# Each scatter of sorted tokens waits for the landing of the scatter before it

## The chip, the cores and the metric

The kernel runs on one core of a Trainium2 chip. It is one launch, and the time is the device time of that launch in microseconds (us). The engines of the core are TensorE (PE in the rows, PEld for its weight loads), VectorE (DVE), ScalarE (ACT), GpSimd (POOL) and SyncE (SP, which here only starts transfers). They run their own instruction streams in order and meet through semaphores.

## The reference: two mixtures of experts, one behind the other

The input x has 8 sequences of 256 tokens with 128 features, all in fp32. Two layers are applied and the result is added to x.

The first layer works by sequence. Each sequence has logits for 8 experts; its two best experts are mixed with softmax weights, and one shared expert is added: gelu(x G) * (x U) times D, with 512 inner features.

The second layer works by token. It is the part that the change touches:

```python
h = (x - mu) / jnp.sqrt(var + LN_EPS) * ln_gamma + ln_beta
sw1, sw2 = (_bit_quant(shared_w1), _bit_quant(shared_w2))      # rounded to -1, 0, 1 times a scale
shared_out = jax.nn.silu(jnp.einsum('btd,fd->btf', h, sw1)) @ sw2.T
probs = jax.nn.softmax(h @ router_w.T, axis=-1)
top_prob, top_idx = jnp.max(probs, axis=-1), jnp.argmax(probs, axis=-1)
h1 = jax.nn.silu(jnp.einsum('btd,efd->ebtf', h, ew1))
eo = jnp.einsum('ebtf,edf->ebtd', h1, ew2)                     # 8 experts, 256 inner features
gate = jax.nn.one_hot(top_idx, N_EXPERTS) * top_prob[..., None]
routed_out = jnp.einsum('ebtd,bte->btd', eo, gate)
```

So every token of the second layer needs one shared expert and the one expert that its router picks.

## The kernel before

**Tiles.** The 2048 tokens are 16 tiles of 128 tokens, one token per partition. The first layer is a row of steps Q (16 for the shared expert, then 4 for each sequence), in which TensorE computes gate and up products (lines 447 to 449), ScalarE the gelu (718), VectorE the product (896) and the split of its result into two fp16 parts (902), and TensorE the down product (477 to 479), three steps later. Work of the second layer is threaded between these steps as the sequences become ready: VectorE's statistics, GpSimd's `deviation` (1270, 1272), ScalarE's `normalise` (764), TensorE's transposes `to_features` (495), ScalarE's features (771), TensorE's logits (502), VectorE's choice of expert (983 to 992). This runs over five parts: three of four tiles, two of two tiles.

**Sorting by expert.** The first 14 tiles go through the routed experts sorted by expert, in two groups: group 0 has tiles 0 to 7, group 1 has tiles 8 to 13. The last two tiles are computed for all eight experts instead (the dense units). For a group, TensorE's `ranks` and VectorE's `sort` give each token a row in a buffer in HBM, `sorted_scratch`, where each expert's rows begin at a multiple of 128; the row numbers are `slot_u` (1022). That buffer has 15 tiles of rows for group 0 and 13 for group 1 and was cleared with zeros early on.

**Scatters.** GpSimd then writes the group's normalised tiles to these rows, one tile with one indirect DMA (`scatter`, line 1275): 8 for group 0, 6 for group 1, each of 128 rows of 512 bytes, 64 KB. All scatters of a group count up one semaphore, by 16 each, and GpSimd issues them one after the other. Between the third and the fourth scatter of group 0 stands `deviation(2)`, behind the last one `deviation(3)`, and behind the last scatter of group 1 `deviation(4)`. Each is in GpSimd's order, so it starts only when GpSimd has got past what is in front of it.

**Loads and units.** SyncE waits until all scatters of a group have landed and loads the sorted rows back in four loads per group (`load_sorted`, line 401), one for each tile unit of three or four sorted tiles. Units 0 to 3 are of group 0, units 4 to 7 of group 1; the buffers of the latter lie in memory that the first layer's weights held, so the rows name them w. TensorE transposes a unit's tiles (`sorted_T`, line 587), ScalarE applies gamma and beta, VectorE splits the result, and TensorE runs the first layer (632), ScalarE the silu (836) and TensorE the second layer (657) with the expert's weights chosen by a register. In TensorE's order the transposes of unit j + 2 stand between the first layer of unit j and the second layer of the unit before it, so those of unit 4 come behind the first layer of unit 2. The transposes of units 0 and 1 come ahead of `ranks(1)`, on which the group 1 row numbers depend.

**Way back.** VectorE copies a unit's result out (1073), SyncE stores it (`store_routed`, 407), behind all eight loads in its order, and GpSimd gathers each tile's rows back with indirect DMAs (1284) when all stores of the group have landed, 8 and then 6. VectorE multiplies them by the gate and adds them (1179) at the very end, after the shared expert's last unit (617) and the four dense units (623, 830, 1085).

```python
            for t in range(GN[0]):
                scatter(0, t)
                if t == 2:
                    deviation(2)
            deviation(3)
            pool.wait_ge(slots_ready, 2)
            pool.wait_ge(norm_done, GP[1])
            for t in range(GN[1]):
                scatter(1, t)
            deviation(4)
```

Of the kernel before, what the change touches and what calls it, by code (L numbers as in the profile page):

```python
# [23 lines left out]
def moe_adaln_ffn(nc, x, cond, g_w, u_w, d_w, sg_w, su_w, sd_w, fs1, fs2, fe1, fe2, router, gamma, beta, out):  # L24
    B, S, D = x.shape
    E, _, I = g_w.shape
    NE, F, _ = fe1.shape
# [29 lines left out]
    NG = 2  # L57
    G0 = [0, 2 * NT]
    GN = [2 * NT, NT + NJ]
# [19 lines left out]
    with ExitStack() as ctx:  # L79
        def sb(name, shape, dt=F32):  # L80
            return ctx.enter_context(nc.sbuf_tensor(name, shape, dt))

        def sem(name):
            return ctx.enter_context(nc.semaphore(name))
# [84 lines left out]
        norm = sb("norm", [P, TT, P])  # L169
# [94 lines left out]
        tiles_ready = sem("tiles_ready")  # L264
        tile_scales = sem("tile_scales")
        cleared = sem("cleared")
        scattered = [sem(f"scattered{g}") for g in range(NG)]
        gathered = [sem(f"gathered{k}") for k in range(len(PIECES))]

        abs_done = sem("abs_done")  # L270
# [59 lines left out]
        def unit_rows(j):  # L330
            _, first, tiles = TILE_UNITS[j]
            return slice(first * P, (first + tiles) * P)
# [10 lines left out]
        def _(sp):  # L343
# [53 lines left out]

            def load_sorted(j):
                g, _, n = TILE_UNITS[j]
                sp.wait_ge(scattered[g], 16 * GN[g])  # L400
                sp.dma_start(hs_sb[j][:, 0:n, :],
                             sorted_dram[g][unit_rows(j)].rearrange("(i p) d -> p i d", p=P)).then_inc(hs_in[j], 16)

# [6 lines left out]
            for j in group_units(0):  # L410
                load_sorted(j)
            sp.wait_ge(out_taken, 2 * B)
            for j in group_units(1):
                load_sorted(j)
# [788 lines left out]
        def _(pool):  # L1203
# [68 lines left out]
                pool.tensor_tensor(shift[:, cols], neg_mean[:, cols], rstd[:, cols], ALU.mult).then_inc(rstd_done, 1)  # L1272

            def scatter(g, t):
                pool.indirect_dma_start(out=sorted_dram[g],  # L1275
                                        out_offset=bass.IndirectOffsetOnAxis(ap=slot_u[g][:, t:t + 1], axis=0),
                                        in_=norm[:, G0[g] + t, :], in_offset=None).then_inc(scattered[g], 16)

            def gather(k):
                g, first, last_tile = PIECES[k]  # L1280
# [18 lines left out]
# [4 lines that stand above are left out]
# [3 lines left out]
            for t in range(GN[1]):  # L1306
                scatter(1, t)
# [25 lines left out]
```

## Time and profile before

| what | value |
|---|---|
| time, median of 2 runs | 195.07 us (193.74 to 196.4) |
| time of the profiled execution | 195.82 us |
| its span | 194.1 us |
| TensorE, matmuls busy | 165.2 us (85%), 1615 instructions |
| VectorE busy | 137.2 us (71%) |
| ScalarE busy | 115.0 us (59%) |
| GpSimd busy | 85.6 us (44%) |
| scatters, line 1275 | 14, 14.9 us busy on GpSimd |
| gathers, line 1284 | 14, 13.3 us busy on GpSimd |
| mean granted TensorE clock | 0.979 of full speed |

The busy share of an engine is an average over stages that differ; it does not say which wait ends last in a given stage. The time of an indirect DMA on GpSimd is that of issuing it. Its data land later, and the row of GpSimd doesn't show that; a transfer that waits for it does, and so does the chain of waits.

### The profile page before, as it was taken

How to read it: one execution, taken by the hardware profiler on the slowest of the kernel's cores; microseconds unless marked ns; L12 is line 12 of the kernel's file. 1: busy time of each engine (PE TensorE's matmuls, PEld its weight loads, DVE VectorE, ACT ScalarE, POOL GpSimd, SP SyncE). 2: the span in 40 equal slices, each digit the busy share in tenths (PEclk: the TensorE clock that was granted, in tenths of full speed). 3: DMA queues.
4: the chain of work that ended last, by engine and by line, in shares of the span. 5: the costliest groups of instructions: out<-in, count | busy, mean ns of one | idle time of the engine just before them, and what ended most of it. 6: DMA issues, size and time to landing. Idle time of an engine off the chain costs nothing.

```text
span 194.1 us, 4961 instructions
## 1 busy us (share of the span) xinstructions
PE 165.2 (85%) x1615; PEld 147.2 (76%) x1615; DVE 137.2 (71%) x350; ACT 115.0 (59%) x281; POOL 85.6 (44%) x139
## 2 busy tenths in 40 slices
PE   0599899999999999899989989879688997559680
PEld 0369799999999999589879977658586996349580
DVE  0328999984689999978999973986753656321474
ACT  4328765664667696787943593855349883353330
POOL 5080000000999867980999766100860007707300
PEclk9999999999999999999999999999969999979998
DMA  3899369998000000000000011700118235231133
GB/s 114 291 340 289 128 203 297 301 341 250 6 14 19 14 17 17 2 19 14 3 14 17 27 30 54 196 12 0 43 41 224 64 96 135 57 95 41 41 113 108
DMA packets 26824, 19.83 MB, mean 102 GB/s; under 512 B 4712, under 2 KB 23536, under 8 KB 26800
## 3 DMA queue, kind: packets, MB, share of 16 engines
q1 hardware_dynamic: 25616, 17.38, 29.8%
q0 software_dynamic: 896, 1.84, 3.4%
q8 instruction: 15, 0.25, 0.5%
q10 hardware_dynamic: 288, 0.30, 0.5%
q14 instruction: 9, 0.07, 0.1%
HBM read 13.28 MB, written 5.64 MB: 97 GB/s over the span
## 4 chain that ended last, share of the span: by engine, by line
PE 37%; DVE 21%; issue 12%; another core or an unknown queue 7%; ACT 7%; DMA 6%; SPq 4%; POOL 3%; DVEq 0%; ACTq 0%; POOLq 0%
DVE a L902 6%; PE ps_out L461 6%; PE ps_up L657 4%; DMA region<-in_L_cond_skill_down 3%; DVE a_sb L896 3%; PE ps_up L447 3%; POOL sorted_scratch L1275 3%; PE ps_up L449 3%; PE ps_up L448 3%; PE ps_gate L447 3%; PE ps_gate L657 3%; PE ps_gate L449 2%; PE ps_gate L448 2%; ACT norm L764 2%
## 5 line engine op out<-in xcount | busy, mean ns | idle before, releaser
L718 ACT ACTIVATE g_sb<-ps_gate 128x512 f32<-128x512 f32 x48 | 28.4, 593 | 26.8 <-PE ps_gate L449 22.5
L896 DVE SCALAR_TENSOR_TENSOR a_sb<-g_sb,mix_w,ps_up 128x512 f32<-128x512 f32 x32 | 23.9, 746 | 10.7 <-PE ps_up L449 3.6
L447 PE MATMUL ps_gate<-x,w 128*128 128x256 f16 x96 | 26.8, 279 | 1.4 <-DVE x L872 1.4
L447 PE MATMUL ps_up<-x,w 128*128 128x256 f16 x96 | 26.8, 279 | 1.4 <-DVE a L896 0.7
L448 PE MATMUL ps_up<-x,w 128*128 128x256 f16 x96 | 26.8, 279 | 0.4 <-issue 0.3
L449 PE MATMUL ps_up<-x,w 128*128 128x256 f16 x96 | 26.8, 279 | 0.0
L448 PE MATMUL ps_gate<-x,w 128*128 128x256 f16 x96 | 26.8, 279 | 0.0
L449 PE MATMUL ps_gate<-x,w 128*128 128x256 f16 x96 | 26.8, 279 | 0.0
L477 PE MATMUL ps_out<-w,a 128*128 x128 | 23.6, 219 | 1.0 <-DVE a L902 0.6
L1284 POOL DMA_INDIRECT routed<-routed_scratch,slot_u x14 | 13.3, 953 | 24.3 <-DMA routed_scratch<-w 20.6
L478 PE MATMUL ps_out<-w,a 128*128 x128 | 23.3, 219 | 0.0
L479 PE MATMUL ps_out<-w,a 128*128 x128 | 23.3, 219 | 0.0
L724 ACT ACTIVATE a<-a_sb 128x512 f16<-128x512 f32 x32 | 20.0, 624 | 5.2 <-DVE a_sb L896 5.2
L866 DVE SCALAR_TENSOR_TENSOR w<-region,w 128x512 f16<-128x512 f32 x26 | 17.4, 682 | 7.6 <-ACT w L702 6.0
L902 DVE TENSOR_TENSOR a<-a_sb,a 128x512 f16<-128x512 f32 x32 | 22.7, 709 | 0.0
L1275 POOL DMA_INDIRECT sorted_scratch<-norm,slot_u x14 | 14.9, 1065 | 13.0 <-DVE slot_u L1022 9.2
L1237 POOL TENSOR_SCALAR scales<-sums 128x3 f32<-128x3 f32 x9 | 2.7, 297 | 36.5 <-ACT abs_junk L753 35.8
L657 PE MATMUL ps_up<-region 128*128 128x128 f32 (+1 forms) x124 | 17.3, 298 | 0.0
L461 PE MATMUL ps_out<-w,a 128*128 128x128 f32 x128 | 16.9, 275 | 0.0
L657 PEld LDWEIGHTS ps_up<-region 128*128 128x128 f32 x124 | 16.6, 215 | 0.2
L836 ACT ACTIVATE region<-ps_gate,tile_scale 128x128 f32<-128x128 f32 x32 | 9.3, 377 | 11.6 <-remote 6.6
L461 PEld LDWEIGHTS ps_out<-w,a 128*128 128x128 f32 x128 | 15.6, 192 | 0.2
(148 smaller groups left out, 403.1 us busy)
## 6 DMA issues: line engine op xcount, KB each, us to landing
region<-in_L_cond_skill_gate SPq DMA_DIRECT2D x8, 256.0 KB, 4.0
region<-in_L_cond_skill_up SPq DMA_DIRECT2D x8, 256.0 KB, 4.4
region<-in_L_cond_skill_down SPq DMA_DIRECT2D x8, 256.0 KB, 5.0
x_tok<-in_x SPq DMA_DIRECT2D x4, 256.0 KB, 6.6
f_raw<-in_L_ffn_expert_w SPq DMA_DIRECT2D x1, 1024.0 KB, 11.2
routed_scratch<-w SPq DMA_DIRECT2D x4, 256.0 KB, 2.6
sorted_scratch<-zeros SPq DMA_DIRECT2D x1, 960.0 KB, 10.5
sorted_scratch<-zeros SPq DMA_DIRECT2D x1, 832.0 KB, 10.3
```

Of the source, the lines that this page charges most:

```text
L447: pe.matmul(dst, w16[:, w_cols(e, 0, col)], x16[:, 0, xs], start=True, stop=False)
L448: pe.matmul(dst, w16[:, w_cols(e, 0, col)], x16[:, 1, xs], start=False, stop=False)
L449: last = pe.matmul(dst, w16[:, w_cols(e, 1, col)], x16[:, 0, xs], start=False, stop=True)
L461: last = pe.matmul(ps_out[batch % 2][:, t * P:(t + 1) * P], a32[:, Q % 4, m * S + t * P:m * S + (t + 1) * P], sd_32[Q % 2][:, m * P:(m + 1 ...
L477: pe.matmul(dst, hi, w16[:, w_cols(e, 0, col)], start=first and t == m == 0, stop=False)
L478: pe.matmul(dst, hi, w16[:, w_cols(e, 1, col)], start=False, stop=False)
L479: last = pe.matmul(dst, lo, w16[:, w_cols(e, 0, col)], start=False, stop=final and t == m == 1)
L657: last = pe.matmul(ps_y[u % 2][:, t * P:(t + 1) * P], s, w, start=c == 0, stop=c == FC - 1)
L718: act.activation(g_sb[:, Q % 2, :], ps_gate[Q % 2][:, :], ACT.Gelu_apprx_tanh, scale=1.0 / WS).then_inc(gelu_done, 1)
L896: dve.scalar_tensor_tensor(out=dst, in0=g_sb[:, Q % 2, :], scalar=weight, in1=ps_up[Q % 2][:, :], op0=ALU.mult, op1=ALU.mult).then_inc(pro ...
L902: dve.tensor_tensor(a16[:, Q % 4, 1, :], a_sb[:, Q % 2, :], a16[:, Q % 4, 0, :], ALU.subtract).then_inc(alo_done, 1)
L1275: pool.indirect_dma_start(out=sorted_dram[g], out_offset=bass.IndirectOffsetOnAxis(ap=slot_u[g][:, t:t + 1], axis=0), in_=norm[:, G0[g] + ...
```

## The change

The one semaphore per group on which the scatters counted becomes two, used in turn: even scatters count on the first, odd ones on the second. Every scatter but the first of a group waits, on GpSimd, until the scatter in front of it has counted its 16, so until that one has landed. SyncE's loads wait for both semaphores of the group, for half of the scatters on each. Nothing else differs; the scatters, their order and their data are the same.

```diff
--- before.py
+++ after.py
@@ -264,7 +264,7 @@
         tiles_ready = sem("tiles_ready")
         tile_scales = sem("tile_scales")
         cleared = sem("cleared")
-        scattered = [sem(f"scattered{g}") for g in range(NG)]
+        scattered = [[sem(f"scattered{g}_{k}") for k in range(2)] for g in range(NG)]
         gathered = [sem(f"gathered{k}") for k in range(len(PIECES))]
 
         abs_done = sem("abs_done")
@@ -397,7 +397,8 @@
 
             def load_sorted(j):
                 g, _, n = TILE_UNITS[j]
-                sp.wait_ge(scattered[g], 16 * GN[g])
+                for k in range(2):
+                    sp.wait_ge(scattered[g][k], 16 * GN[g] // 2)
                 sp.dma_start(hs_sb[j][:, 0:n, :],
                              sorted_dram[g][unit_rows(j)].rearrange("(i p) d -> p i d", p=P)).then_inc(hs_in[j], 16)
 
@@ -1272,9 +1273,12 @@
                 pool.tensor_tensor(shift[:, cols], neg_mean[:, cols], rstd[:, cols], ALU.mult).then_inc(rstd_done, 1)
 
             def scatter(g, t):
+
+                if t >= 1:
+                    pool.wait_ge(scattered[g][(t - 1) % 2], 16 * ((t - 1) // 2 + 1))
                 pool.indirect_dma_start(out=sorted_dram[g],
                                         out_offset=bass.IndirectOffsetOnAxis(ap=slot_u[g][:, t:t + 1], axis=0),
-                                        in_=norm[:, G0[g] + t, :], in_offset=None).then_inc(scattered[g], 16)
+                                        in_=norm[:, G0[g] + t, :], in_offset=None).then_inc(scattered[g][t % 2], 16)
 
             def gather(k):
                 g, first, last_tile = PIECES[k]
```

## Rows read from the trace of the kernel before

**Rows 1.** The page, part 4: the ended-last chain by line, share of the span.

```profile
DVE a L902 6%; PE ps_out L461 6%; PE ps_up L657 4%; DMA region<-in_L_cond_skill_down 3%; DVE a_sb L896 3%; PE ps_up L447 3%; POOL sorted_scratch L1275 3%; PE ps_up L449 3%; PE ps_up L448 3%; PE ps_gate L447 3%; PE ps_gate L657 3%; PE ps_gate L449 2%; PE ps_gate L448 2%; ACT norm L764 2%
```

**Rows 2.** Chain of waits, 142 to 148 us: start us, us, what.

```profile
142.39 2.24 DMA sorted_scratch<-norm,slot_u
...
144.69 3.00 DMA w<-sorted_scratch
...
147.74 0.33 PE ps_out L587
```

**Rows 3.** TensorE's time line: start, us, engine, line, instruction, count [idle before <-releaser].

```profile
115.43 0.44 PE L495 MATMUL ps_b<-ident,norm 128*128 128x128 f32 x2 [0.52 <-ACT norm L764]
...
131.82 1.07 PE L587 MATMUL ps_out<-ident,hs_sb 128*128 128x128 f32 x8
...
141.36 0.94 PE L632 MATMUL ps_up<-region 128*128 128x128 f16 x8 [1.52 <-issue]
...
142.73 3.00 PE L657 MATMUL ps_up<-region 128*128 x16
...
146.96 0.67 PE L632 MATMUL ps_up<-region 128*128 128x128 f16 x8 [0.26 <-ACT region L836]
...
148.24 1.95 PE L657 MATMUL ps_gate<-region 128*128 x16
```

**Rows 4.** Busy us by stretch: PE, PEld, DVE, ACT, POOL, then granted clock, DMA.

```profile
141.00:147.00 6.00, 5.08 (x36) 4.67 (x37) 3.52 (x11) 3.25 (x11) 2.95 (x4) 0.72 0.28 86
147.00:153.00 6.00, 5.79 (x57) 5.28 (x58) 2.71 (x5) 5.79 (x19) 0.00 (x0) 1.00 0.66 181
```

**Rows 5.** GpSimd's time line, group 0 scatters.

```profile
107.12 1.38 POOL L1275 DMA_INDIRECT sorted_scratch<-norm,slot_u  x1 [0.31 <-POOL f_raw L1261]
...
112.35 1.05 POOL L1270 TENSOR_TENSOR rstd<-var_e,neg_half 128x4 f32<-128x4 f32 x1 [1.18 <-DVE neg_mean L970]
113.47 0.20 POOL L1272 TENSOR_TENSOR shift<-neg_mean,rstd 128x4 f32<-128x4 f32 x1
...
117.70 1.48 POOL L1275 DMA_INDIRECT sorted_scratch<-norm,slot_u  x1 [0.30 <-issue]
119.49 0.96 POOL L1275 DMA_INDIRECT sorted_scratch<-norm,slot_u  x1 [0.30 <-issue]
125.26 0.73 POOL L1270 TENSOR_TENSOR rstd<-var_e,neg_half 128x2 f32<-128x2 f32 x1 [4.82 <-DVE neg_mean L970]
```

**Rows 6.** GpSimd's time line, group 1 scatters, first and last of six.

```profile
135.75 1.03 POOL L1275 DMA_INDIRECT sorted_scratch<-norm,slot_u  x1 [9.20 <-DVE slot_u L1022]
...
142.39 0.96 POOL L1275 DMA_INDIRECT sorted_scratch<-norm,slot_u  x1 [0.30 <-issue]
```

**Rows 7.** SyncE's DMA queue, time line, the group 0 loads.

```profile
121.77 2.02 SPq L401 DMA_DIRECT2D hs_sb<-sorted_scratch  x4
```

**Rows 8.** VectorE's time line.

```profile
117.66 0.69 DVE L1061 TENSOR_TENSOR region<-h_all,region 128x512 f16<-128x512 f32 x1
...
135.29 0.17 DVE L1022 TENSOR_SCALAR slot_u<-slot_f 128x6 uint32<-128x6 f32 x1
...
189.98 1.66 DVE L1179 SCALAR_TENSOR_TENSOR x_tok<-routed,prob,x_tok 128x128 f32<-128x128 f32 x6
```

**Rows 9.** Chain of waits, pieces without a known releaser.

```profile
118.35 2.85 another core or an unknown queue
...
161.64 3.77 another core or an unknown queue
...
167.54 3.82 another core or an unknown queue x2
...
178.78 3.27 another core or an unknown queue
```

**Rows 10.** The loads of group 0's sorted tiles, issue to landing.

```profile
DMA to landing us min/median/max: 3.0/3.7/4.0
```

**Rows 11.** GpSimd's time line, the last gather.

```profile
181.12 0.95 POOL L1284 DMA_INDIRECT routed<-routed_scratch,slot_u  x1 [0.30 <-issue]
```

## The prediction

> **What bounds the kernel now.** I read the page first. Its chain by line is a list of many VectorE and TensorE lines, and one entry is the scatter itself, "POOL sorted_scratch L1275 3%" [rows 1]. So the line that the change touches is on the path that ends last; the next question is where. I then read the chain of waits in order of time around the group 1 scatters [rows 2]. It runs without a gap from the last scatter: issued at 142.39 us, landed 2.24 us later, SyncE starts the load of sorted tokens at 144.69, that load lands 3.00 us later, and TensorE's transposes of that unit start at 147.74. TensorE had finished the work in front of them a moment earlier (146.96 + 0.67 = 147.63 [rows 3]), and everything for the remaining units is queued behind them. So whatever makes the last scatter of group 1 land later comes out at TensorE one for one. After 147.74 TensorE has hardly any idle time (5.79 of 6 us busy [rows 4]), and from there the chain goes through the units one after the other to the end. Nothing in it waits for a clock time, so a delay at 147.74 is not given back by itself.
>
> The time lines of GpSimd give the scatters' beat [rows 5, 6]. An undisturbed scatter keeps GpSimd 0.96 us and the next starts 0.30 us after that, one every 1.27 us, while the last one needs 2.24 us from its start to its landing [rows 2]. Today the landing of one overlaps the issue of the next.
>
> **The price of one wait.** With the change, scatter t starts when scatter t-1 has landed, plus the time that GpSimd needs to wake and start. The landing: 2.24 us [rows 2]; group 0 confirms it, its last scatter starts at 119.49 and the load that waits for it at 121.77, 2.28 us later [rows 5, 7]. The start after a wait: slot_u ends at 135.29 + 0.17 = 135.46 and the scatter that waited for it starts at 135.75 [rows 8, 6], 0.29 us. So a beat is 2.24 + 0.29 = 2.53 us in place of 1.27, 1.26 us more. Bounds: 0.97 us if the start is already prepared when the landing comes (2.24 - 1.27), and 1.78 us if each scatter also takes 1.48 us instead of 0.96, as the slow one at 117.70 did [rows 5] (1.26 + 0.52). I take 1.26: 10 of the 14 scatters lie within 0.1 us of 0.96.
>
> **Group 1, on the path.** Six scatters, five waits. Today they start from 135.75 to 142.39, 6.64 us apart in all [rows 6]. Then 5 x 2.53 = 12.65 us, so the last starts and lands 6.0 us later, and load and transposes follow. No cover: TensorE waits for this load already [rows 2, 3]. With the two bounds: 5 x 2.24 - 6.64 = 4.6 us, and 5 x 3.05 - 6.64 = 8.6 us.
>
> **Group 0, beside the path except at one point.** Seven waits. The first scatter takes 1.38 us, 0.42 more than the others, so the third starts at 107.12 + 0.42 + 2 x 2.53 = 112.6 and leaves GpSimd at 113.56. In GpSimd's order the reciprocal deviation of part 2 (line 1270) is queued behind the third scatter. Today it waits for VectorE and starts at 112.35 [rows 5]; then it starts at 113.56, 1.2 us later. ScalarE's normalise needs its result, the shift that ends at 113.67 today, and TensorE's transposes of part 2 wait 0.52 us for that normalise at 115.43 [rows 5, 3]. Both are queued in front of the last expert work, so 1.2 us goes to TensorE here and on to the group 1 slots. Bounds: 0 (the slip vanishes in the 2.85 us that this chain later spends on "another core or an unknown queue" [rows 9]) and 1.7 (a third scatter of 1.48 us). I take 1.2.
>
> The rest of group 0 is hidden. Scatter 3 starts 0.29 us behind the shift, at 113.67 + 1.2 + 0.29 = 115.16, the last 4 x 2.53 later at 125.28, and lands at 127.5 against 121.7 today. The loads follow; landing takes 3.7 us in the median and 4.0 at most [rows 10], so unit 0's tokens are there at 131.3. What hides it is the last work of the expert layers: TensorE comes to these transposes at 131.82 [rows 3], then at 133.0 with the slip. If that cover were gone, up to 5.8 us would be on the path. The deviation of part 3, queued behind the last scatter, would find GpSimd free at 126.24; its input from VectorE comes at 125.26 today [rows 5] and 126.4 with the slip, so it adds nothing. The deviation of part 4, behind the last scatter of group 1, goes to the dense tiles, whose transposes stand behind the stalled unit on TensorE: nothing.
>
> **SyncE.** Each of the eight loads has one more wait, on a semaphore that is already full when the other one is; I cost it at nothing, between 0 and the 0.06 us that lie today between landing (142.39 + 2.24 = 144.63) and issue (144.69) [rows 2]. The routed stores stand behind the group 1 loads on SyncE and are late with them, but the gathers wait for the last store of a group, whose data come from the delayed TensorE anyway. The last gather leaves GpSimd at 182.07 [rows 11] and, with a scatter's 1.28 us from there to the landing, is in at 183.4; VectorE wants it at 189.98 [rows 8], and both sides move together: nothing.
>
> **TensorE's clock.** The stall at the group 1 transposes grows from 0.1 to about 6 us. What holes can do is in the trace: behind TensorE's idle 1.52 us before 141.36, the stretch 141 to 147 has a mean granted clock of 0.72, so part of it ran at 1.2 GHz instead of 2.4, and the same 16 matmuls took 3.00 us there and 1.95 us in the next unit [rows 3, 4]. I expect one further slow stretch behind the new stall. Price: 3.00 - 1.95 = 1.05 us for the second-layer matmuls of a unit, and up to 0.3 for a half of the first layer (0.94 against 0.67). Part of the slow time may fall into the stall, so I take 1.0; bounds 0 and 1.9.
>
> **The sum.** 6.0 + 1.2 + 1.0 = 8.2 us. The profiled execution took 195.82 us (its span 194.1) and would take 204.0; the median of the two runs is 195.07, 0.75 us lower, so the forecast is 203.3 us.
>
> A rule of the Trainium skill speaks against the change: "DMA: Bandwidth & Descriptors", section "Rules for kernel authors", advises to issue a transfer early, compute, and wait late, since the fixed cost then overlaps. The trace agrees, with 1.27 us a scatter against 2.24 for a landing. The same page, section "Anatomy of one DMA — SWDGE (gpsimd) path", fits 2.0 us plus bytes over 436e3; for 64 KB that gives 2.15 us, an estimate by which group 1 would cost 5.5 us and the forecast be 202.8.
>
> **Rivals.**
>
> *A, the forecast* (203.3 us).
>
> *B, the slip of group 0 is swallowed.* Before 121.2 the chain holds 2.85 us of unexplained waiting while scatters are being issued [rows 9, 5]. If scatters one at a time disturb the other engines less, this shrinks, and then the group 1 slots are bound by unit 1's tokens: 127.6 + 0.5 + 4.0 = 132.1, its transposes end at 132.6, against 131.82 + 1.07 = 132.9 today. So 6.0 - 0.3 + 1.0 = 6.7 and 201.8 us. For it: the wait has no releaser in the trace. Against: no such wait is seen at the first five scatters either.
>
> *C, slow scatters.* The scatter at 117.70 took 1.48 us while VectorE subtracted two SBUF tiles from 117.66 on [rows 5, 8]. Today this is half hidden; in a serial row every such delay is paid. At 0.52 us each, group 1 costs 2.6 us more (205.9); group 0's five scatters behind the deviation put its tokens at 133.9, 0.9 past their cover: 206.8 us. Against: most scatters ran undisturbed beside VectorE's work. The Trainium skill, "SBUF — State Buffer", section "Who interferes with whom", says that a VectorE instruction with two inputs in SBUF and a GpSimd instruction that reads SBUF lock each other out; by that rule this rival would be the usual case in group 0.
>
> *D, the other side: the units behind the stall lose their unexplained waits.* From 161 to 182 the chain has 3.77 + 3.82 + 3.27 = 10.9 us on "another core or an unknown queue", ScalarE waiting while GpSimd issues gathers [rows 9, 11]. They are larger than the whole cost, and I can't say what makes them. If the shifted meeting of stores, gathers and units removed them all, 203.3 - 10.9 = 192.4 us. It decides from 4.3 us removed (203.3 - 199.0); with the 2.85 us of group 0 gone too, 189.6, which would be faster. Against: gathers and units move by the same delay, so they meet as before.
>
> *E, the change does not do what it says*: each landing is over before the next scatter could start anyway, 195 us. The 2.24 us against the beat of 1.27 excludes it, unless that landing is the last one's alone.
>
> **How the numbers follow.** Chances: A 0.53, B 0.16, C 0.12, D 0.17, E 0.02. What a measurement of this kernel can tell from no change is about 2%, 191.2 to 199.0 us; the two runs shown differ by 1.4%. A with its own bounds (4.6 to 8.6, 0 to 1.7, 0 to 1.9) covers 199.7 to 207.3. The range goes from 199.0 to 207.5 and holds A, B and C, leaving out D and E, 0.19. Slower by over 2%: A, B, C, 0.81. Faster: the extreme of D, 0.04. Within 2%: the rest, 0.15.
>
> **What the profile after would show.** GpSimd's scatters 2.4 to 2.6 us apart in both groups, each ended by a DMA landing; line 1270 of part 2 at about 113.6; the first group 0 load at 127.5 with no TensorE wait at its transposes; the last group 1 scatter 12.6 us after the first; TensorE idle about 6 us in front of the transposes of unit 4, released by the load; a stretch at the lower clock right behind it; the units from there to the end as long as today. The prediction fails if the beat is below 2.2 us, if TensorE waits at unit 0 already, or if the stretch from unit 4 to the end changes by more than 3 us.

## The result: 209.25 us, slower, and above the range

The changed kernel took 209.25 us in the median of 2 runs (207.88 to 210.63) against 195.07 us: a ratio of 1.070, with a 95% interval of 1.063 to 1.076. The direction was right and the size was not; 203.3 us was forecast, 207.5 at most. Ratios and intervals, here and below, are worked out from the fast runs of both kernels and medians from all runs, so a ratio can differ a little from the quotient of two medians. The profiled execution took 210.63 us, with a span of 208.8, so 14.7 us more than the span of 194.1 before. The two runs are a thin base: in later sets of six runs the same kernel was 1.042 and 1.039 times as long as the one before.

**The scatters on GpSimd's time line**, columns as in [rows 5]; they answer to [rows 5, 6]:

```profile
106.98 1.38 POOL L1279 DMA_INDIRECT sorted_scratch<-norm,slot_u  x1 [0.31 <-POOL f_raw L1262]
...
112.58 0.96 POOL L1279 DMA_INDIRECT sorted_scratch<-norm,slot_u  x1 [1.54 <-DMA sorted_scratch<-norm,slot_u]
113.56 1.06 POOL L1271 TENSOR_TENSOR rstd<-var_e,neg_half 128x4 f32<-128x4 f32 x1
...
122.88 1.48 POOL L1279 DMA_INDIRECT sorted_scratch<-norm,slot_u  x1 [2.51 <-DMA sorted_scratch<-norm,slot_u]
127.63 0.96 POOL L1279 DMA_INDIRECT sorted_scratch<-norm,slot_u  x1 [3.27 <-DMA sorted_scratch<-norm,slot_u]
130.14 0.96 POOL L1279 DMA_INDIRECT sorted_scratch<-norm,slot_u  x1 [1.55 <-DMA sorted_scratch<-norm,slot_u]
131.13 0.73 POOL L1271 TENSOR_TENSOR rstd<-var_e,neg_half 128x2 f32<-128x2 f32 x1
...
141.74 1.03 POOL L1279 DMA_INDIRECT sorted_scratch<-norm,slot_u  x1 [9.61 <-DVE slot_u L1023]
...
154.39 0.96 POOL L1279 DMA_INDIRECT sorted_scratch<-norm,slot_u  x1 [1.53 <-DMA sorted_scratch<-norm,slot_u]
```

Each scatter now waits for a landing. In group 1 the first and the last are 12.65 us apart, to the hundredth what was forecast. In group 0 the last one starts at 130.14 us instead of the forecast 125.28, and the deviation of part 3 behind it at 131.13.

**The chain of waits** (start us, us, what), where it enters the scatters and where it leaves them; it answers to [rows 2]:

```profile
112.58 3.63 DMA sorted_scratch<-norm,slot_u
...
116.49 2.31 DMA sorted_scratch<-norm,slot_u
...
119.07 3.54 DMA sorted_scratch<-norm,slot_u
...
122.88 4.49 DMA sorted_scratch<-norm,slot_u
...
131.13 0.74 POOL rstd L1271
...
141.28 0.18 DVE slot_u L1023
...
154.39 2.23 DMA sorted_scratch<-norm,slot_u
...
156.71 2.75 DMA w<-sorted_scratch
```

What the reader is to see: the chain goes through group 0's scatters as well, which it didn't before, and three of their landings take 3.5 to 4.5 us instead of 2.3. From the last scatter it goes by the deviation, ScalarE's normalise, TensorE and VectorE to group 1's row numbers. The page's chain by line says the same in one entry, against 3% for the scatters in [rows 1]:

```profile
DMA sorted_scratch<-norm,slot_u 13%; PE ps_gate L658 7%; PE ps_out L462 6%; PE ps_up L658 5%; DVE a L903 4%; DMA region<-in_L_cond_skill_down 3%; PE ps_up L448 2%; PE ps_up L450 2%; PE ps_up L449 2%; PE ps_gate L448 2%; PE ps_gate L449 2%; PE ps_gate L450 2%; POOL sorted_scratch L1279 2%; PE ps_out L588 2%; DVE a_sb L897 2%
```

**TensorE's time line**, answering to [rows 3]; in brackets its idle time and what ended it:

```profile
133.10 0.44 PE L496 MATMUL ps_b<-ident,norm 128*128 128x128 f32 x2 [4.16 <-ACT norm L765]
134.86 1.01 PE L618 MATMUL ps_gate<-region 128*128 128x512 f16 x2 [1.32 <-ACT region L827]
...
137.23 1.95 PE L588 MATMUL ps_out<-ident,hs_sb 128*128 128x128 f32 x8
138.97 0.25 PE L525 MATMUL ps_b<-chosen_e,earlier 128*128 128x56 f16 x1
...
159.50 1.12 PE L588 MATMUL ps_out<-ident,w 128*128 128x128 f32 x4 [9.29 <-DMA w<-sorted_scratch]
160.41 3.62 PE L658 MATMUL ps_gate<-region 128*128 x16
...
165.27 1.95 PE L658 MATMUL ps_up<-region 128*128 x16
```

TensorE is idle for 4.16 us ahead of part 3's transposes, where no hole was forecast, and for 9.29 us ahead of unit 4's. Behind each hole the matmuls take nearly twice their time: the second layer of a unit 3.62 us and later 1.95, the eight transposes of sorted tokens 1.95 us against 1.07 in [rows 3]. In the kernel before, part 3's transposes and the start of `ranks(1)` (524 there, 525 here), on which group 1's row numbers depend, are these rows:

```profile
128.81 0.39 PE L495 MATMUL ps_b<-ident,norm 128*128 128x128 f32 x2
...
133.06 0.20 PE L524 MATMUL ps_b<-chosen_e,earlier 128*128 128x56 f16 x1 [0.18 <-DVE chosen_e L992]
```

From the one to the other it is 4.25 us before and 5.87 after (133.10 to 138.97), at a mean granted clock of 1.00 before and 0.54 after. The stretch around the second hole, columns as in [rows 4] (the granted clock stands ahead of the DMA share):

```profile
154.00:159.50 5.50, 0.00 (x1) 0.00 (x1) 0.00 (x0) 0.88 (x2) 1.89 (x3) 0.50 0.33 98
159.50:165.00 5.50, 5.50 (x35) 5.44 (x36) 0.94 (x2) 1.00 (x2) 0.00 (x0) 0.57 0.43 118
165.00:173.00 8.00, 8.00 (x89) 7.97 (x88) 4.46 (x13) 7.45 (x25) 0.00 (x0) 1.00 0.35 93
173.00:209.00 36.00, 24.13 (x177) 21.48 (x174) 15.54 (x45) 11.36 (x31) 13.42 (x14) 0.85 0.28 79
```

While TensorE has nothing to do the grant is 0.50, the 1.2 GHz level; in the 5.5 us after it the mean is 0.57, and only then full speed. In the last 36 us the mean is 0.85: there are slow stretches again.

**Where the 14.7 us are**, by the same four points in both spans:

| stretch | before | after | difference |
|---|---|---|---|
| to `slot_u` of group 1 | 135.29 | 141.28 | +6.0 |
| first to last scatter of group 1 | 6.64 | 12.65 | +6.0 |
| from the last scatter to unit 4's transposes | 5.35 | 5.11 | -0.2 |
| unit 4's transposes to the end of the span | 46.4 | 49.3 | +2.9 |

The sum of the rows, with 0.46 us between `slot_u` and the first scatter in both, is the difference of the spans. SyncE's queue shows the group 0 loads, which answer to [rows 7]:

```profile
132.44 2.02 SPq L402 DMA_DIRECT2D hs_sb<-sorted_scratch  x4
```

They start 10.7 us later than in [rows 7], and VectorE's row numbers, in the chain above at 141.28, 6.0 later than in [rows 8].

### The profile page after: what moved, and what is told of

The parts are those of the page before. It is cut to its first block, busy times and chain, and to the rows that moved or that the text cites. A ratio compares the mean times of both kernels' runs of the same rounds, so it can differ in the third digit from the quotient of the medians.

```text
span 208.8 us, 4968 instructions
## 1 busy us (share of the span) xinstructions
PE 168.8 (81%) x1615; PEld 151.7 (73%) x1615; DVE 136.9 (66%) x350; ACT 115.3 (55%) x281; POOL 85.5 (41%) x139
## 4 chain that ended last, share of the span: by engine, by line
PE 45%; DMA 18%; DVE 16%; issue 10%; SPq 4%; ACT 3%; POOL 3%; DVEq 0%; POOLq 0%
DMA sorted_scratch<-norm,slot_u 13%; PE ps_gate L658 7%; PE ps_out L462 6%; PE ps_up L658 5%; DVE a L903 4%; DMA region<-in_L_cond_skill_down 3%; PE ps_up L448 2%; PE ps_up L450 2%; PE ps_up L449 2%; PE ps_gate L448 2%; PE ps_gate L449 2%; PE ps_gate L450 2%; POOL sorted_scratch L1279 2%; PE ps_out L588 2%; DVE a_sb L897 2%
## 5 line engine op out<-in xcount | busy, mean ns | idle before, releaser
L658 PE MATMUL ps_gate<-region 128*128 128x128 f32 (+1 forms) x116 | 18.6, 327 | 0.0
L658 PEld LDWEIGHTS ps_gate<-region 128*128 128x128 f32 x116 | 18.0, 241 | 0.5 <-issue 0.3
L658 PE MATMUL ps_up<-region 128*128 128x128 f32 (+1 forms) x124 | 16.5, 289 | 0.0
```

The lines of the kernel that those rows point to most:

```text
L658: last = pe.matmul(ps_y[u % 2][:, t * P:(t + 1) * P], s, w, start=c == 0, stop=c == FC - 1)
```

## Why some landings are slow

In the trace a scatter is 32 packets, 16 of 4096 bytes and 16 of 4 bytes, and it has landed when the last of them has. The DMA queues of two short stretches of the changed kernel, each around a slow landing, against one around an ordinary landing (queue and kind: packets, MB, share of 16 engines). At 113.8 to 115.6 us, the third scatter (3.63 us):

```profile
q0 software_dynamic: 32, 0.07, 12.2%
q8 instruction: 1, 0.02, 4.3%
```

At 124.6 to 126.9 us, the sixth (4.49 us, of which 1.48 for issuing it):

```profile
q0 software_dynamic: 32, 0.07, 9.6%
q8 instruction: 1, 0.02, 4.4%
```

At 127.6 to 129.6 us, the seventh, landed in 2.2 us:

```profile
q0 software_dynamic: 32, 0.07, 10.2%
```

Beside each slow landing there is one packet of an engine's own instructions on the DMA engines (for the fifth scatter, 3.54 us, one of queue 14), and beside the ordinary one there is none. In each of the three slow scatters 30 of the 32 packets start within 0.34 us; the other two, one of 4096 and one of 4 bytes, come later, the last of them 1.4, 1.0 and 1.8 us after the first. Over all 14 scatters of the profiles of the changed kernel, the kernel before and the sixteen runs below, 252, it is the same: in 213 the last packet started 0.33 to 0.43 us after the first, and no instruction packet overlapped any of them; in 39 it started 0.49 us or more after, and an instruction packet overlapped every one. While the landings are hidden behind the next issue this costs nothing. One of the 39 is in the trace of the kernel before, the third scatter of group 1 (138.59 us), beside an instruction packet at 139.93, and no row of the prediction has it; in a serial row each one is paid in full. The Trainium skill, "Runtime: NRT & Kernel Launch", section "Instruction fetch mechanics", says that an engine's sequencer fetches 16 KiB blocks over a DMA queue of its own and that the cost of crossing into the next block is mostly hidden. The trace agrees on the block for queue 8 (15 packets carry 0.25 MB); what such a fetch costs another transfer that something waits for, the section doesn't say, and here it is 1.4 us for the third scatter (3.63 for 2.24).

## The experiments

One thing has to be known to read the times. The kernel before takes 186 us in three of the sets of runs and 195 to 197 in the other one and in the first comparison. Each of the four sets ran on a chip of its own, so these are called faster and slower chips below; whether it is the chip or the moment isn't shown. A profile of it from a slower chip has stretches of 2.6 to 3.9 us in the chain that end with no known releaser, 14.1 us together; the profiles of its nearest relatives from the faster chips (with `ranks(1)` moved, and with two scatters in flight) have none. So every kernel here is compared only with the kernel before on the same chip.

### Which group costs what

In `scatter`, the wait in one group only; the loads wait as in the changed kernel.

```diff
-                if t >= 1:
+                if g == 1 and t >= 1:
```

> Waits in group 1 only. Theory Q (the wait is dear in group 0 because GpSimd's deviation of part 3 is queued behind the last scatter, and group 0's landings are slower than 2.24 us): the last scatter of group 1 starts 12.65 us after the first instead of 6.64, and TensorE's hole in front of unit 4 grows from 0 to 6 us and is followed by a stretch at the lower clock. 6.0 + 1 to 1.9, so 202 to 203 us. Theory H (the prediction: group 0 is hidden but for 1.2 us) expects the same here. Theory N (each wait costs the same, wherever it is): 5 of 12 waits, 14.2 x 5/12 = 5.9, so 201.0 us.

192.04 us against 186.41, ratio 1.036 (1.029 to 1.043). GpSimd's time line:

```profile
134.33 1.03 POOL L1279 DMA_INDIRECT sorted_scratch<-norm,slot_u  x1 [9.86 <-DVE slot_u L1023]
...
146.93 0.96 POOL L1279 DMA_INDIRECT sorted_scratch<-norm,slot_u  x1 [1.54 <-DMA sorted_scratch<-norm,slot_u]
```

12.60 us from the first to the last: the same row as in the changed kernel, and 5.6 us of cost by the medians, 5.3 to 7.9 by the interval. The term of 6.0 us for group 1 holds. Whether the clock adds 1 to 1.9 us the interval leaves open, and this run alone doesn't tell theory N (5.9 us) from the others; the next one does.

```diff
-                if t >= 1:
+                if g == 0 and t >= 1:
```

> Waits in group 0 only. Theory Q: the last scatter of group 0 starts at 128 to 130 us, the deviation of part 3 behind it, TensorE waits 3 to 4 us for the normalise of part 3, group 1's row numbers come 4.5 to 6 us late: 199.5 to 201.5 us. Theory H: 1.2 us late, 196.3 us. Theory N: 7 of 12 waits, 8.3 us, 203.4 us.

189.52 us against 186.41, ratio 1.017 (1.009 to 1.024): 3.1 us, 1.7 to 4.5 by the interval. Theory N (8.3) is out, the 1.2 us of the prediction are too few, and the 4.5 to 6.5 of theory Q begin at the edge. It was run again on a chip of the slower kind:

> Waits in group 0 only, once more: its runs lay from 188.2 to 192.6 us. Theory Q: the spread comes from how many of group 0's landings are slow, 0 to 4 of them by 0.6 to 1.9 us each, so the runs fall anywhere from 188 to 193 and not into two narrow heaps; together with the 5.6 to 6.6 us of group 1's waits it makes up the whole loss of the changed kernel, 12 to 14 us. If the groups' losses overlapped (one hidden behind the other), the changed kernel would lose less than their sum by more than 2 us.

198.02 us against 196.83, ratio 1.010 (1.005 to 1.016): 1.2 us by the medians, 2.0 by the ratio. So group 0 costs something on both chips, but not the 6 us of the first profile, and the 12 to 14 us expected for both groups together didn't come. On the faster chips the two groups add up to 5.6 + 3.1 = 8.7 us by the medians, and the changed kernel lost 8.7 in the last set; by the ratios it is 9.7 against 7.2, so that they overlap somewhat isn't excluded.

### The deviation that stands behind the last scatter

If GpSimd's order is what group 0 costs, the deviation of part 3 ought to be put ahead of the last two scatters.

```diff
                 if t == 2:
                     deviation(2)
-            deviation(3)
+                if t == 5:
+                    deviation(3)
```

> The changed kernel, with the deviation of part 3 moved from behind the last scatter of group 0 to behind the sixth. Theory Q: it starts when GpSimd comes to it, at about 124.5 us instead of 131.1, TensorE's 4.2 us wait for the normalise of part 3 goes away, and the next bound appears: the transposes of units 0 and 1 need the loads, which land at about 136.4, and the ranks of group 1 are queued behind them. Group 1's row numbers at about 139 instead of 141.3: 206 to 207.5 us. If the queue place of the deviation were the whole of it: 204. Theory H: no change, 209.2.

197.27 us against 186.41, ratio 1.065 (1.056 to 1.073). The changed kernel wasn't in that set; its ratios elsewhere are 1.039 to 1.070, so no gain is to be seen. The deviation did start at 124.58 us instead of 131.13. TensorE's time line shows what was late next:

```profile
134.16 1.97 PE L588 MATMUL ps_out<-ident,hs_sb 128*128 128x128 f32 x8 [2.21 <-DMA hs_sb<-sorted_scratch]
135.92 0.25 PE L525 MATMUL ps_b<-chosen_e,earlier 128*128 128x56 f16 x1
```

The tokens of units 0 and 1 depend on the last scatter too, and their transposes stand ahead of `ranks(1)` (525) in TensorE's order. One row of scatters had two ways to the row numbers, and only one was shortened. The next kernel closes both:

```diff
+            ranks(1)
             sorted_T(0)
             sorted_T(1)
-            ranks(1)
```

> As the one before, and in TensorE's order the ranks of group 1 moved in front of the transposes of units 0 and 1. Theory Q: nothing of group 0's row is in front of group 1's row numbers any more; they come at about 134 to 135.5 us, as in the kernel before, and only the price of group 1 is left, 201.5 to 203.5 us. If a large part of the loss lay in something else of group 0 (the loads of its own tiles), 206 or more would be left.

193.95 us against 186.41, ratio 1.042 (1.034 to 1.050), 3.3 us less than with the early deviation alone. TensorE's time line:

```profile
133.15 0.20 PE L525 MATMUL ps_b<-chosen_e,earlier 128*128 128x56 f16 x1 [1.10 <-DVE chosen_e L993]
...
134.35 0.66 PE L588 MATMUL ps_out<-ident,hs_sb 128*128 128x128 f32 x4 [0.87 <-DMA hs_sb<-sorted_scratch]
```

`ranks(1)` now waits for VectorE alone and the slots of group 1 come at 135.38 us, 2.9 us earlier than with the early deviation alone, while the last scatter of group 0 is as late as before (129.11). It was run beside the changed kernel itself:

> All waits in place, the deviation of part 3 behind the sixth scatter and the ranks ahead of the transposes. Theory Q: group 1's row numbers come at the time of the kernel before (134 to 136), whatever group 0's landings do; what is left is 6.0 for group 1's row and 1 to 3.5 for the clock and the holes behind: ratio 1.035 to 1.05. If group 0 cost nothing in the changed kernel either (its typical run), the changed kernel's ratio is the same; if it costs 2 to 6 us, the changed kernel's is 1.01 to 1.03 above this one.

194.15 us, against 194.82 of the changed kernel and 186.12 of the kernel before: ratio 1.043 (1.038 to 1.047). Its slots come at 135.22 us, 1.5 earlier than the changed kernel's 136.74 there, but the medians can't be told apart. So the two ways through group 0 are shown in the traces of these kernels; their worth in time isn't beyond what six runs resolve.

The order of ranks and transposes by itself, in the kernel before:

> The kernel before, without any of the waits, with the ranks of group 1 in front of the transposes of units 0 and 1 on TensorE. They no longer stand behind 1.07 us of transposes. If group 1's row numbers are on the path, as the chain says: 0.7 to 1.1 us faster, 194.0 to 194.4 us. If the transposes' delay is passed on to unit 0 and from there to unit 2 instead: 195.

185.36 us against 186.24, ratio 0.994 (0.991 to 0.997), 10 runs; and once more:

> The kernel before with the ranks of group 1 ahead of the transposes of units 0 and 1: 0.5 to 1.1 us faster than the kernel before, ratio 0.994 to 0.998, on whichever chip it is.

185.34 us against 186.12, ratio 0.994 (0.991 to 0.996), 12 runs. This version beats both kernels: the one before by 0.8 to 0.9 us by the medians and 1.1 to 1.2 by the ratios, small but the same twice.

### One landing deeper

Scatter t waits for scatter t-2, with the same semaphores and one wait fewer per group.

```diff
-                if t >= 1:
-                    pool.wait_ge(scattered[g][(t - 1) % 2], 16 * ((t - 1) // 2 + 1))
+                if t >= 2:
+                    pool.wait_ge(scattered[g][t % 2], 16 * (t // 2))
```

> The two semaphores and the waits stay, but each scatter waits for the one before the one in front of it, so two are in flight. A landing takes 2.24 to 2.7 us from the start and the next but one starts 2.54 us after it anyway. Theory Q: as good as the kernel before, 194.5 to 197 us, a little more only where a landing comes late (3.6 to 4.5 us). Rival (the waits themselves, as instructions on GpSimd and SyncE, or the second semaphore cost the time): near 209.

187.59 us against 186.24, ratio 1.007 (1.003 to 1.011), 10 runs. GpSimd's time line in group 1:

```profile
134.46 1.03 POOL L1279 DMA_INDIRECT sorted_scratch<-norm,slot_u  x1 [9.87 <-DVE slot_u L1023]
135.80 1.20 POOL L1279 DMA_INDIRECT sorted_scratch<-norm,slot_u  x1 [0.30 <-issue]
137.30 0.96 POOL L1279 DMA_INDIRECT sorted_scratch<-norm,slot_u  x1 [0.30 <-issue]
139.63 0.96 POOL L1279 DMA_INDIRECT sorted_scratch<-norm,slot_u  x1 [1.37 <-DMA sorted_scratch<-norm,slot_u]
```

Ten waits and both semaphores are there, the row is 7.70 us (the last scatter starts at 142.16) instead of 12.65, and nearly the whole loss is gone: about 1.3 us are left. What costs is that only one scatter is in flight, not the wait instructions or the second wait in SyncE's loads. One of group 1's four waits held GpSimd up, by 1.07 us ahead of 139.63. It waited for the scatter of 135.80, which had taken 3.6 us to land, again with an instruction packet in that stretch.

### TensorE's clock behind the hole

36 matmuls whose result nobody reads keep TensorE at work in the hole ahead of unit 4's transposes.

```diff
+                if u == TU[2]:
+                    for i in range(36):
+                        pe.matmul(ps_a[:, :], earlier[:, :], x16[:, 0, 0:512], start=True, stop=True)
                 if u in TU and u + 2 in TU:
                     sorted_T(TU.index(u + 2))
```

> The changed kernel with 36 matmuls of 512 columns in fp16, whose result nobody reads, on TensorE in front of the transposes of unit 4, about 7.7 us of its 9.3 us hole. If the lower clock behind the hole costs what the rows say (3.62 against 1.95 us for the second layer of unit 1, 1.12 against 0.66 for the transposes), the time falls by 1.5 to 2.2 us, to 207 to 207.7. If the clock's loss is hidden behind other engines: 209.2.

194.49 us against 186.24, ratio 1.041 (1.034 to 1.048). The changed kernel wasn't in that set, so this alone says nothing of the clock. The set on a chip of the slower kind has both:

> The changed kernel itself, on the chip of the experiments, where the kernel before takes 186.3 us and no wait of 3 us without a releaser is left behind 160 us. Theory Q adds up from parts that don't need those waits: group 1 6.0, group 0's delay of the row numbers 6 to 7, lower clock 1 to 2, so 198.5 to 200.5 us and a ratio near 1.07. If the unexplained waits of the first chip took part in the loss, less: 195 to 197.

206.32 us against 196.83, ratio 1.042 (1.036 to 1.049). The expected ratio near 1.07 didn't come, nor did the faster chip that it was worked out for.

> The filled kernel once more, beside the changed kernel on the same chip. Its time below that of the changed kernel is the price of the clock behind TensorE's hole: 1.5 to 2.5 us by the second layer and transposes of that unit, 0 if other engines hide it, and 4 or more if the lower clock also slows the units behind.

205.16 us, ratio 1.044 (1.038 to 1.050). TensorE's time line of the filled kernel:

```profile
157.17 0.66 PE L588 MATMUL ps_out<-ident,w 128*128 128x128 f32 x4 [1.37 <-DMA w<-sorted_scratch]
157.66 1.95 PE L658 MATMUL ps_gate<-region 128*128 x16
```

and the same two groups of the changed kernel on that chip:

```profile
154.25 1.11 PE L588 MATMUL ps_out<-ident,w 128*128 128x128 f32 x4 [9.88 <-DMA w<-sorted_scratch]
155.16 3.07 PE L658 MATMUL ps_gate<-region 128*128 x16
```

With the hole filled the unit runs at full speed, and from there to the end it takes 46.1 us; with the hole 50.7. The kernel before has 47.0 there. So filling the hole was worth 4.6 us of this stretch in these profiles. The medians don't show it, because the filled kernel came to unit 4 already 2.9 us later, with its slots at 138.82 against 135.98 us. Its group 0 row ended later (127.63 against 126.00), which put part 3's transposes on TensorE 1.2 us later (130.64 against 129.44); and behind the longer hole there, 1.67 us against 0.42, the clock was low, so the way to `ranks(1)` took 5.87 us against 4.32. On the faster chips this end takes 37.2 us in the changed kernel and 36.4 and 37.4 in the two profiles of the kernel before with its ranks moved, so there the hole costs less than 1 us. In the changed kernel on a faster chip the grant is 1.00 from 160 to 190 us; on the slower one it is 0.83 from 158 to 204 us. Of the 4.6 us above, 3.9 are TensorE's busy time, 38.0 us against 34.1 for the same 295 matmuls, more than the one slow stretch behind the hole explains; there are further slow stretches near the end on that chip. Why one chip has them and another not is open.

For comparison, the kernel before once more in that set, as a measure of the noise (its expectation still had the faster chip in mind):

> The kernel before, for its trace on this chip: 186.3 us, the same scatters (first of group 0 at 107, first of group 1 at 134.4 to 135.8), and none of the waits of 3.3 to 3.8 us behind 160 us.

197.04 us, ratio 1.003 (0.999 to 1.008). Its chain of waits has this piece beside group 0's scatters, the like of [rows 9]:

```profile
117.16 3.86 another core or an unknown queue
```

### Moving the instruction packets

If slow landings are made by instruction packets, other places of these packets make other scatters slow. Extra matmuls at TensorE's start, with results that nobody reads, push its instruction stream along. First 24 in fp32:

```diff
             pe.wait_ge(const_done, 1)
+            for i in range(24):
+                pe.matmul(ps_out[0][:, 0:32], ident[:, :], ident[:, 0:32], start=True, stop=True)
             x_transpose(0)
```

> The changed kernel with 24 small matmuls (48 instructions with their weight loads), whose result nobody reads, on TensorE at the very start, while it waits for the input. The idea under test: the three slow landings of group 0 (3.63, 3.54 and 4.49 us instead of 2.3 to 2.7) come from instruction fetches of 16 or 8 KB that sit on one DMA engine just when that engine has a packet of the scatter. Then the fetches for TensorE move 1.5 to 2 us ahead, to about 112.2 and 123 us, other scatters or none are hit, and the two hit now land in 2.3 to 2.8 us: 206 to 208.5 us. If the slow landings belong to the scatters (their rows, their place): the same three are slow, 209 to 210.

200.35 us against 186.24, ratio 1.072 (1.063 to 1.081). The matmuls took 10.45 us and put the first scatter at 112.4 instead of 107 us, so the time says nothing of the packets. The slow landings did move, to the second and the seventh scatter, beside instruction packets at 116.7 and 130.9 us. Then 32 small ones in fp16; behind the diff stands first the changed kernel of the same set:

```diff
+            ident16 = ident[:, :].bitcast(F16)
+            for i in range(32):
+                pe.matmul(ps_out[0][0:32, 0:16], ident16[:, 0:32], ident16[:, 0:16], start=True, stop=True)
```

> The changed kernel once more. Group 0's last scatter starts between 126 and 130.5 us, by 1 to 3 slow landings. Ratio 1.04 to 1.07 (8 to 13 us).

194.82 us against 186.12, ratio 1.039 (1.033 to 1.044).

> The changed kernel with 32 tiny fp16 matmuls (64 instructions with their weight loads), whose result nobody reads, on TensorE at the start while it waits for the input; they should cost under 0.5 us. TensorE's instruction stream is fetched 16 KB at a time, so its fetches come 2 to 2.7 us earlier: about 111.5 and 122 us instead of 113.9 and 124.7. If fetches make the landings slow: the third scatter of group 0 (started at 112.6) lands in 2.2 to 2.4 us instead of 2.9 to 3.9, and whichever scatter has its packets out at 111.5 or 122 is slow instead, or none; the ratio to the kernel before is 1.03 to 1.055. If the slow landings belong to the scatters: the third is slow again.

196.28 us, ratio 1.052 (1.047 to 1.058). The first scatter stands at 106.96 us, so the matmuls cost nothing here. The two instruction packets of queue 8 came at 112.08 and 123.10 us, against 112.88 and 126.68 in the changed kernel of that set; about 111.5 and 122 were expected. The chain of waits at the third scatter, in this kernel:

```profile
112.56 0.96 POOL sorted_scratch L1282
...
113.55 1.07 POOL rstd L1274
...
115.10 2.31 DMA sorted_scratch<-norm,slot_u
```

and in the changed kernel of that set:

```profile
112.38 2.97 DMA sorted_scratch<-norm,slot_u
...
115.63 2.31 DMA sorted_scratch<-norm,slot_u
```

The DMA queues of the shifted kernel at 113.5 to 115.2 us:

```profile
q0 software_dynamic: 32, 0.07, 12.0%
```

No instruction packet, no slow landing: the chain leaves the third landing and goes through the deviation instead, as the prediction had it. The packet at 112.08 us was over at 113.4, before the scatter's first at 114.1. In the ten profiles with group 0's waits and TensorE's start unchanged the third scatter has a late packet in nine, and in those nine the instruction packet overlaps it. That is the mechanism, moved by hand, in one profile. It made the kernel no faster: in the profiles the slots come at 136.76 and 136.74 us, since the last scatter started at the same time (125.89 and 126.02 us); the sixth took 1.49 us to issue and the seventh 1.10, where the packet's delay had been. The median is even 1.5 us higher, in stretches that I could not tie to the edit; that stays open.

## Why the prediction was wrong, step by step

**Right.** The beat: 2.53 us forecast, 2.50 to 2.57 in group 1. Group 1 on the path: 6.0 us forecast and measured, and 5.6 us with its waits alone. SyncE's waits: nothing, as forecast; issue and landing of the unit 4 load were even 0.2 us shorter together. The gathers as well: the last one starts at 195.19 us, 9.5 ahead of VectorE's use of it at 204.71, against 8.9 in [rows 11, 8]. Rival E is out by the beat. Rival D is out by the result, though its premise came true in part: ScalarE's waits without a releaser between unit 4 and the end went from 11.9 to 3.7 us, yet TensorE's idle time there went only from 13.0 to 11.7, and the time got longer. None of the three signs by which the prediction said it would fail came: the beat is 2.5 us, TensorE doesn't wait at unit 0 (no idle time ahead of 137.23), and the end changed by 2.9 us and not by more than 3. It failed where it had no sign.

**The step that failed** is "The rest of group 0 is hidden", with its deviation of part 3 that "adds nothing". It rested on two numbers 0.2 us apart: GpSimd free at 126.24 us, VectorE's input at 126.4. Both were off, in opposite directions. The input was there at 124.47 (VectorE's `neg_mean`, 124.31 + 0.16), because the unexplained wait of 2.85 us ahead of it [rows 9] did not come; that is rival B's premise. And GpSimd was free at 131.10 (130.14 + 0.96). The term for group 0 was 1.2 us with 1.7 as its upper bound, and measured 6.0. None of the 6.0 is the slip that the 1.2 stood for. That slip came as forecast, `rstd` of part 2 at 113.56 and its transposes on TensorE at 116.65 instead of 115.43, but the last down product before part 3 starts at 128.72 against 128.75 before, so it was swallowed on the way, as rival B had it. The 6.0 are 4.3 us that part 3's transposes start late (133.10 against 128.81), and 1.6 us that TensorE takes longer from there to `ranks(1)` (5.87 against 4.25), because it runs at the lower clock behind that hole. The prediction gave no slow stretch to group 0.

How near the step was depends on the landings. In the slower chip's set the last scatter of the changed kernel started at 126.00 us, 0.7 after the forecast, TensorE's hole ahead of part 3 was 0.42 us, the clock stayed at full speed there, and the slots came only 0.2 us later than in the kernel before there, which had an unexplained wait of 3.86 us of its own beside the scatters. The queue order and the low clock turn a late row into lost time; the late landings make the row late.

**Why the row was longer.** 125.28 was forecast for the last scatter and 130.14 measured, 4.9 us. The third, fifth and sixth scatters account for it: their distances to the next ones were 3.91, 3.81 and 4.75 us, against 2.56 (112.6 to 115.16, the deviation included) and twice 2.53, so 1.35 + 1.28 + 2.22 = 4.85 us. Of the fifth 0.34 and of the sixth 0.52 is a slow issue (1.30 and 1.48 for 0.96), as in rival C; the rest, 4.0 us, is landings beside instruction packets. I priced a landing by the undisturbed one, 2.24 us, and took the lateness of a scatter only from its issue; the landings of the middle ones were in no row, and I should have put a spread on them rather than one value.

**The clock.** 1.0 us was forecast with 1.9 as the upper bound, and the end of the span grew by 2.9. The second layer behind the hole took 3.62 us, 1.67 more than 1.95, where 1.05 was taken from the shorter hole in [rows 3]; the transposes of that unit add 0.46 (1.12 for 0.66), and 0.8 is left. The hole was 9.29 us and not the forecast 6, since TensorE got through units 0 to 3 faster than before, without the idle and slow stretch of [rows 3, 4]. Nor was it the one further slow stretch: from unit 4 to the end the mean grant is 0.85 against 0.95 before, and TensorE is busy 37.6 us against 33.3 with the same 295 matmuls, 4.3 more, while it is idle 1.4 less. The 2.9 can't be put on the clock alone: the end of the span holds waits of the unexplained kind in both traces, 3.77 + 3.82 + 3.27 us before [rows 9], and in the changed kernel this one, on ScalarE's time line:

```profile
178.95 1.14 ACT L837 ACTIVATE region<-ps_gate,tile_scale 128x128 f32<-128x128 f32 x4 [3.71 <-remote]
```

That the hole makes the slow stretch is shown by filling it. That the hole costs time is shown for the slower kind of chip and in profiles only (50.7 against 46.1 us); how much of this 2.9 us it is stays open.

**How sure the size is.** The 14.2 us come from two runs each. Three measurements of the changed kernel give +14.2 (2 runs), +9.5 (6) and +8.7 us (6). By the ratios these are 13.6, 8.3 and 7.2 us. The share of group 0 is what varies: its slots are 6.0 us late in the first profile, 0.2 in that of the second set against the kernel before there (135.98 and 135.78 us), and in the third 2.7 to 2.9 (136.74 us against 133.87 in the kernel with waits in group 1 only and 134.00 in the one with two in flight, on other faster chips). The sum of 8.2 us was close to the later two, and that is luck: its parts were 6.0, a slip that was swallowed, and a clock that costs less than 1 us on the faster chips. Which of the three a reader should expect I can't say; what decides it, the place of instruction packets, slow issues and the unexplained waits, is in no row that the prediction used.

## What to carry to other kernels

A queue of small transfers on one engine costs its issue beat while several are in flight and its full landing when they go one at a time; two in flight give nearly all of it back. A serial chain pays for every slow member that overlap had hidden, so price it with the spread of the landings and not with the undisturbed one. When two events arrive within the error of the estimate, treat the later path as open: name both ways to the next point, and check which engines' queue orders make a third. A wait that opens a hole on TensorE can be paid a second time behind it, at the lower clock: look at every hole, the small ones too (here 1.6 us behind part 3's).

## What the runs showed of the hardware

- An indirect scatter of 64 KB from GpSimd takes 0.96 us to issue, about 0.57 to its first packet, 0.34 for the packets and 0.37 to the signal, 2.24 in all. With one instruction packet of 8 or 16 KB beside it, its last packets come late and it took 2.8 to 3.8 us, and 4.29 and 4.49 in two cases together with a slow issue.
- The issue is slow only beside VectorE's work: the 33 scatters that overlapped no VectorE instruction took 0.95 to 1.04 us, the 24 that overlapped the subtraction `region<-h_all,region` of two SBUF tiles 0.96 to 1.48, 1.35 in the median. That the one makes the other wasn't tested.
- The wait itself costs GpSimd nothing that shows: a scatter starts 0.27 us after the landing that it waits for, and 0.30 after the one before it when it waits for none.
- The same kernel in different sets of runs, each on a chip of its own: 186 us, or 195 to 197 us with waits of 2.6 to 3.9 us that have no releaser in the trace, most of them in stretches in which GpSimd issues indirect transfers. What makes them was not found.
